# A gated attention and feed-forward block on one core: the product with V in groups of four head pairs, and a second norm in place

## The reference

```python
# attention: query = layernorm(x), key = value = context
q, k, v = proj(layernorm(x), Wq, bq), proj(ctx, Wk, bk), proj(ctx, Wv, bv)
q, k = q * cos + rotate_half(q) * sin, k * cos + rotate_half(k) * sin
scores = where(|i - j| <= 50, q @ k.T / 4, -1e9)
p = softmax(scores)
x = x + tanh(g_xattn) * ((p @ v) @ Wo.T + bo)
# feed-forward, every tensor rounded by a scale from its own maximum
n = layernorm(x)
x = x + tanh(g_ffn) * qdq(qdq(silu(qdq(n @ Wg.T))) * qdq(n @ Wu.T)) @ Wd.T
```

## Time and profile before

| what | value |
|---|---|
| median of three executions | 1368.07 us |
| profiled execution, its own time | 1368.83 us |
| its span (first to last instruction) | 1367.10 us |
| attention with its start and end | 0 to 809 us |
| feed-forward | 809 to 1367 us |
| TensorE busy | 88% of the span |
| VectorE busy | 89% |
| ScalarE busy | 60% |
| GpSimd busy | 40% |
| mean granted TensorE clock | 0.965 of full speed |

### The profile page before, as it was taken

How to read it: one execution, slowest core, us unless ns; L and a number is a source line. 1 busy time by engine, 2 the same in 40 slices (tenths; PEclk the granted TensorE clock), 3 DMA queues, 4 the chain that set the end, 5 groups by cost and what they waited for, 6 DMA issues and landing times. The chain is left out here.

```text
span 1367.1 us, 27802 instructions
## 1 busy us (share of the span) xinstructions
PE 1203.8 (88%) x8963; PEld 786.5 (58%) x8995; DVE 1212.9 (89%) x3603; ACT 826.5 (60%) x1336; POOL 549.5 (40%) x1357
## 2 busy tenths in 40 slices
PE   5689898989998988998988659998999799968998
PEld 3457666666666666666666434443433334427887
DVE  3799999999999999999998849997999989988886
ACT  2255656666666665656565536665677599983332
POOL 1177777777777777777776610000000000000000
PEclk9699999999999999999999869999999999988999
DMA  2757575757565666666664202223455455546764
GB/s 78 156 121 183 135 174 139 168 139 164 143 161 146 158 151 153 154 151 158 146 161 112 102 8 93 111 97 127 158 183 185 159 191 196 199 165 205 241 225 169
DMA packets 132369, 207.27 MB, mean 152 GB/s; under 512 B 11159, under 2 KB 97050, under 8 KB 126106
## 3 DMA queue, kind: packets, MB, share of 16 engines
q1 hardware_dynamic: 132250, 205.86, 54.4%
HBM read 125.60 MB, written 79.69 MB: 150 GB/s over the span
## 5 line engine op out<-in xcount | busy, mean ns | idle before, releaser
L670 DVE CUSTOM_DVE_ANT_0 psum<-psum,band 128x178 f32<-128x178 f32 x1024 | 316.5, 372 | 38.4 <-PE psum L878 38.1
L552 ACT ACTIVATE probs<-psum 128x356 f32<-128x356 f32 x512 | 210.6, 468 | 162.7 <-PE psum L895 162.2
L486 POOL TENSOR_SCALAR_AFFINE_SELECT probs<-probs 128x154 f32<-128x154 f32 (+1 forms) x512 | 221.4, 443 | 156.5 <-ACT probs L552 150.5
L1088 PE MATMUL psum<-xnT,w_upT 128*128 (+1 forms) x1152 | 261.1, 384 | 19.0 <-DVE maxima L1312 8.8
L1088 PEld LDWEIGHTS psum<-xnT,w_upT 128*128 128x128 f16 x1152 | 109.9, 99 | 170.0 <-issue 32.6
L878 PE MATMUL psum<-k_stack,q_stack 96*128 96x178 bf16 x1024 | 141.3, 245 | 51.3 <-DVE smax L670 47.4
L495 POOL TENSOR_SCALAR_AFFINE_SELECT probs<-probs 128x254 f32<-128x254 f32 (+1 forms) x512 | 180.3, 375 | 0.0
L895 PE MATMUL psum<-q_stack,k_stack 98*128 98x178 bf16 x1024 | 136.2, 242 | 16.8 <-DMA q_stack<-shiftT 10.5
L670 DVE DVE_READ_ACCUMULATOR2_ANT smax<- 128x1 f32 x1024 | 142.9, 140 | 0.0
L1688 PE MATMUL psum<-w_downT,xnT 128*128 128x256 f16 x1152 | 128.3, 275 | 16.0 <-DVE xnT L1638 16.0
L878 PEld LDWEIGHTS psum<-k_stack,q_stack 96*128 96x128 bf16 x1024 | 74.2, 98 | 109.0 <-DVE smax L670 87.2
(11 more groups left out here) (189 smaller groups left out, 2265.3 us busy)
## 6 DMA issues: line engine op xcount, KB each, us to landing
k_parts_scratch<-k_parts SPq DMA_DIRECT2D x32, 384.0 KB, 2.5
q_parts_scratch<-q_parts SPq DMA_DIRECT2D x32, 384.0 KB, 2.6
k_stack<-k_parts_scratch SPq DMA_DIRECT2D x32, 384.0 KB, 5.1
q_stack<-q_parts_scratch SPq DMA_DIRECT2D x32, 384.0 KB, 7.3
gate_scratch<-g_stage SPq DMA_DIRECT2D x16, 768.0 KB, 3.2
g_in<-gate_scratch SPq DMA_DIRECT2D x16, 768.0 KB, 4.6
sig_scratch<-w_gateT SPq DMA_DIRECT2D x32, 384.0 KB, 2.3
sig_again<-sig_scratch SPq DMA_DIRECT2D x32, 384.0 KB, 3.4
```

The source lines that it names most:

```text
L486: nc.gpsimd.affine_select(out=t[:, :, 0:n], in_=t[:, :, 0:n], pattern=[[0, 2], [1, n]], compare_op=ALU.is_ge, fill=0.0, base=WINDOW - off, ...
L552: nc.scalar.activation(ring_tile(probs, b, pair, c)[:].rearrange("p e j -> p (e j)"), scoreT_bank[c][:, 0:2 * SPAN], ACT.Exp, scale=DK ** ...
L670: ins = nc.vector.tensor_tensor_reduce(out=mine, in0=mine, in1=keep["band"][:, t, :], scale=1.0, scalar=-3e38, op0=ALU.add, op1=ALU.max, a ...
L1088: last = nc.tensor.matmul(bank[:], weights[wp][:, c * I + f * P:c * I + (f + 1) * P], x_parts[:, c, bass.ds(j * (2 * TILE) + xp * TILE, TI ...
```

## The change

The ring of probability tiles grows from 8 to 12. `weigh` is called at the end of slots 3 and 7 alone, for four pairs each time: pairs 4 to 7 of b3 in slot 3, pairs 0 to 3 of b2 in slot 7. The second norm is written over x2 instead of into xn2, which is dropped; so ScalarE waits for the store of x2 before it, TensorE transposes x2, and the refill of an x2 buffer waits for that transposition instead of the norm.

```diff
-RING = 8
+RING = 12
...
-        xn2 = sb("xn2", [P, T, D])
...
-                reached(sp, x2_normed, bb, T, T)
+                reached(sp, x2_transposed, bb, 1, 1)
...
                         reached(act, x2_transposed, b4.before(1), 1, 1)
-                        normalise(b4, x2[b4.buf], xn2, scale2, scale2_ready, x2_normed)
+                        loaded(act, x2_stored, b4)
+                        normalise(b4, x2[b4.buf], x2[b4.buf], scale2, scale2_ready, x2_normed)
...
-                        transpose4(bank_b, xn2[:].rearrange("p t d -> p (t d)")).then_inc(x2_transposed, 1)
+                        transpose4(bank_b, x2[b4.buf][:].rearrange("p t d -> p (t d)")).then_inc(x2_transposed, 1)
...
-                    if slot % 2 == 1:
-                        for back in (1, 0):
+                    if slot % 4 == 3:
+                        for back in (3, 2, 1, 0):
                             pair, late = pair_at(slot - back, PV_FIRST)
                             weigh(Batch(rnd, unit, late), pair, b2)
```

## The result

The changed kernel took 1396.71, 1388.49 and 1393.24 us, median 1393.24, against 1368.07 before: ratio 1.0163, 95% interval [1.0122, 1.0205]. It is slower, by about what was forecast (1389.4, range 1379 to 1397). Measured again twice beside the experiments it took 1393.60 and 1393.56 us.

What follows compares the result with a forecast made beforehand. VectorE's work plus TensorE's too-long chain from slot 7 to slot 0 bounds each iteration; 17.4 + 3.6 + 0.5 less 0.15 gives +21.35 us, 1390.2 on the profiled execution, so median 1389.4 us, range 1379 to 1397.

Steps and rivals of the forecast that it cites:

- The bound: Steady attention: an iteration is VectorE's own 21.5 us plus 1.00 us by which TensorE's slot 7 to slot 0 chain is too long.
- The product with V in slot 7: Slot 7: four pairs instead of two lengthen the chain and VectorE's slot 0 wait by 0.60 us per iteration (0.45 to 0.75).
- rival C: Four pairs run as two groups, the second half waiting for the first: slot 7 costs 0.75 us or more, 1393.8; chance 0.10.
- Slots 1, 3 and 5: Groups of 0.75 us leaving slots 1 and 5 gain nothing; four pairs in slot 3 cost nothing, with 1.5 us cover on VectorE.
- Rivals A: The too-long chain begins in slot 5, so the group leaving there pays back slot 7: 1363.7 us, not slower; chance 0.05.
- B: TensorE is the bound throughout: 64 fewer groups each save 0.15 us of entry and exit, 1358.5 us, faster; chance 0.05.
- rival D: Slot 3 overruns its cover, so slot 4's scores come late and VectorE waits a second time: 1395 us or more; chance 0.03.
- The store of x2: Second norm on ScalarE waits for this store: nothing in steady iterations, 0 to 1.8 us in iteration 33, taken as 0.5.
- Half clock: Slot 3 of iterations 3, 32 and 34: four more steps at half TensorE clock cost 1.2 us each, 3.6 us together.
- less 0.15: Iteration 34: a group leaves slot 1 (0.75 us) and one is lengthened in slot 7 (0.60) ahead of a waiting weight.
- the sum: Whole kernel: 17.4 us from slot 7, 3.6 half clock, 0.5 store, less 0.15 in iteration 34, together +21.35 us.
- main term: Slot 7's longer group over iterations 4 to 31 and 33: 29 x 0.60 = 17.4 us.

Runs made afterwards that it cites:

- the faster version with the store still behind the weights: Changed kernel with no product with V in slot 7, its group of four in slot 3, first half's turning ahead of the Wq projection: 1355.05 us, ratio 0.9895.

## Why the prediction was right, point by point

**The bound.** Right. The chain from slot 7's scores to slot 0's scores sets the pace with VectorE's own work. Four pairs in slot 3 or 0.65 us of extra work in slot 5 cost nothing in steady iterations, about as much in slot 7 costs all of it. One reading was loose: of the 17 waits in the earlier trace rows 15 are the wait of 1.0 us, one for each iteration, and two are of under 0.2 us; that changes nothing.

**The product with V in slot 7.** Predicted 0.60 us in each iteration; the group itself grew by 0.62 and VectorE's wait by 0.63. Over 29 iterations that is 18.3 us against 17.4. A group of four takes 1.37 us, less than two groups of 0.75, so there is no stop inside it, and rival C falls.

**Slots 1, 3 and 5.** Right: no gain from the groups that left, TensorE's wait behind slot 5 went to 1.13 us (predicted 1.1), and the waits for maxima in slot 7 stayed at 0.21 and 0.27. Rivals A and B needed these waits to be none. The scores of slot 4 still wait 0.48 us for maxima, where the prediction had this wait all but used up; it shrank to 0.08 us only in the version with four pairs in slot 3 alone. VectorE did not wait there in either, so rival D falls. As for the rule of the Trainium skill behind B (TensorEngine Tiling (Array Packing), Key Properties: changing the tiling mode drains the engine): 1.37 us for four pairs against 2 x 0.75 for two groups does save 0.13 us, so the trace agrees with a cost of entry and exit; it was saved where TensorE waits anyway.

**The store of x2.** Predicted 0.5 us in iteration 33. In the profiled execution of the changed kernel the term did not show: the store was issued at 783.7 and landed 7.3 us later, at 791.0, and the norm, held up by slot 3's group at half clock, started at 791.94.

```profile
788.01 2.62 PE L921 MATMUL psum<-probs,V 128*32 128x178 f32 x32
...
791.94 1.10 ACT L527 ACTIVATE x<-x,ln_scale 128x256 f32<-128x256 f32 x2
```

With the norm in place alone it was a wait of 1.17 us, and in the faster version with the store still behind the weights 3.25 us: the sooner ScalarE arrives, the longer it waits.

**Half clock.** Predicted 3.6 us for slot 3 of iterations 3, 32 and 34. The mechanism was right: 2.62 us busy for 32 records instead of 1.44, 1.2 us more, as computed. But it was one place too few, since in the profiled execution slot 3 of iteration 33 ran at half clock too. From the residual of iteration 31 to that of 35 it took 86.6 us instead of 81.4, 5.2 us more; the terms for them come to 3.95 (2 x 0.60, 2 x 1.2, 0.5, less 0.15).

**What was missing.** The falls of the clock in steady iterations. I took the full clock of the rows before as given, while making TensorE's idle time in slot 5 three times as long. The profiled execution took 27.9 us more where the sum has 21.35. Up to the residual of iteration 4 it lost 2.5 us (the sum has 1.2), with a fall of the clock at 103.8 us that the kernel before did not have. From there to iteration 31 it lost 19.7 (16.2): 17.2 by the pace and most of the rest by three falls of 0.9 us each. From iteration 31 to 35 it lost 5.2 (3.95), and after that 0.3 (0).

The medians of 1393.24 to 1393.60 us lie about 4 us above the forecast. Only profiled executions show where the clock fell; the two others of the changed kernel had one fall each in the steady part and one near 103 us. So the falls are part of these 4 us, how large a part is not shown. They do not explain the spread of the executions either: the kernel before had none in its profiled execution and spreads from 1364.47 to 1373.31 us. The forecast thus has its mechanism and its main term, 17.4 of 21.35 us, shown by the runs. Its small terms were partly wrong both ways, the store too high, the half clock and the falls too low, and the closeness of the last few microseconds is partly luck.

## What to carry to other kernels

Before merging or moving work on a busy engine, find the one wait of the pacing engine and follow it back to the last instruction that itself had to wait. In this kernel work between these two points cost its full time (0.62 us in each iteration by the group, 0.85 by three idle matmuls), and work where the engine waited anyway cost nothing. A merge that saves a little at each switch loses if it gathers work in that stretch; the same group in slot 3 is free. In slot 1 it was not: there it made VectorE wait 0.41 us, so a place is free only as far as its own cover reaches. After such a move look at once for the waits that take the old one's place, and at the granted clock in each stretch, since it can fall where it did not before.

## What the runs showed of the hardware that I had not expected

The granted clock fell to half for some 3.5 us though TensorE's longest single wait just before was only 1.1 us. It had been busy for 2.34 of 3.5 us in the changed kernel, and for 2.42 of 3.9 us in the first version without the product in slot 7. The same stretch an iteration earlier (2.34 and 2.41 us busy) was followed by the full clock in both. In the profiled executions there were none to three falls in iterations 4 to 31, and 12 in that one version, where they cost more (12 x 1.6 us) than the shorter wait in slot 0 gave (28 x 0.56 us). The idle time before a fall is thus not enough to foresee one; a forecast of a kernel with such stretches should allow for a few of them.
